# Sending each token of two mixture layers to its own expert, in blocks of 64, through DRAM

## The reference

```
x = x + _L0_gnn_ref(xn, ...) + _L0_mix_ref(xn[None], ...)[0]
x = x + _L0_ffn_ref(_layernorm(x), ...)          # mixture, erf gelu, bias on the logits
...
x = x + _L2_gnn_ref(...) + _L2_mix_ref(...)
x = x + _L2_ffn_ref(_layernorm(x), ...)          # mixture, silu

def _L0_ffn_ref(x, Ws, bs, W1, b1, W2, b2):      # E = 8 experts, D = 768, F = 384, 512 tokens
    logits = xt @ Ws + bs
    probs = jax.nn.softmax(logits, axis=-1)
    routes, prob_max = jnp.argmax(probs, -1), jnp.max(probs, -1)
    h = gelu(jnp.einsum('td,edf->etf', xt, W1) + b1[:, None, :], approximate=False)
    y = jnp.einsum('etf,efd->etd', h, W2) + b2[:, None, :]
    out = jnp.take_along_axis(y, routes[None, :, None], axis=0)[0]
    return out * prob_max[:, None]
```

## Time and profile before

| | |
|---|---|
| median of three runs | 5067.96 us (5066.04 to 5071.9) |
| the profiled execution | 5071.08 us, its span 5069.0 us |
| TensorE busy | 4789.0 us, 94% |
| VectorE busy | 980.5 us |
| ScalarE busy | 988.2 us |
| granted TensorE clock, mean | 0.967 |
| DMA | 716.13 MB, 141 GB/s over the span |

### The profile page before, as it was taken

The page is one execution under the profiler, slowest core; times in us unless marked ns, Lnnn a source line. Parts: engine busy times, 40 slices in busy tenths (PEclk is TensorE's granted clock), DMA queues, the critical chain, the costliest instruction groups (busy, mean ns, idle before and its releaser), DMA issues.

```text
span 5069.0 us, 39557 instructions
## 1 busy us (share of the span) xinstructions
PE 4789.0 (94%) x15392; PEld 2191.0 (43%) x15410; DVE 980.5 (19%) x1791; ACT 988.2 (19%) x1796; POOL 54.1 (1%) x91
## 2 busy tenths in 40 slices
PE   8999999999999998998999999999779999999998
PEld 6544444444444544443444444444333433333343
DVE  3782111212101133212300000010443100000000
ACT  0121112323201425331210101010541111010010
POOL 1000000000000000000000000000000000000000
PEclk9999999999899998999999999989889999999999
DMA  3013222121232121012203030323104899999998
GB/s 115 1 39 103 75 70 73 52 71 58 62 100 75 46 67 33 25 50 83 71 31 102 29 99 32 105 72 99 29 25 148 344 410 423 411 424 410 417 414 358
DMA packets 110479, 716.13 MB, mean 141 GB/s; under 512 B 13200, under 2 KB 13392, under 8 KB 71552
## 3 DMA queue, kind: packets, MB, share of 16 engines
q1 hardware_dynamic: 103104, 670.21, 35.6%
q0 software_dynamic: 5216, 25.34, 1.3%
q10 hardware_dynamic: 2016, 18.49, 0.9%
HBM read 707.18 MB, written 6.82 MB: 141 GB/s over the span
## 4 chain that ended last, share of the span: by engine, by line
PE 88%; DVE 4%; DMA 4%; ACT 3%; issue 1%; SPq 0%; ACTq 0%; DVEq 0%
PE bank L392 80%; DMA mem<-in_experts 4%; PE bank L546 3%; PE bank L513 2%; PE bank L390 2%; DVE rstd L1715 1%; DVE mem L1950 0%; ACT mem L1402 0%; DVE mem L1946 0%; ACT mem L1557 0%; ACT mem L1423 0%; DVE mem L1718 0%; ACT mem L1123 0%; DMA mem<-in_edges 0%; ACT mem L1265 0%
## 5 line engine op out<-in xcount | busy, mean ns | idle before, releaser
L392 PE MATMUL bank<-mem 128*128 128x512 f32 (+5 forms) x11616 | 3942.9, 568 | 115.9 <-DMA mem<-in_experts 25.9
L392 PEld LDWEIGHTS bank<-mem 128*128 128x128 f32 (+3 forms) x11616 | 1668.8, 172 | 2320.9 <-issue 2160.2
L1123 ACT ACTIVATE mem<-bank,cols 128x512 f32<-128x512 f32 (+1 forms) x139 | 95.5, 687 | 975.5 <-PE bank L392 975.5
L390 PE MATMUL bank<-ident,mem 128*128 128x128 f32 (+2 forms) x1300 | 200.2, 309 | 59.2 <-ACT mem L1402 9.9
L390 PEld LDWEIGHTS bank<-ident,mem 128*128 128x128 f32 (+2 forms) x1300 | 167.9, 160 | 151.6 <-issue 91.4
L1123 ACT ACTIVATE mem<-bank 128x512 f32<-128x512 f32 x168 | 99.5, 597 | 551.6 <-PE bank L392 547.0
L546 PE MATMUL bank<-mem 128*128 128x512 bf16 x798 | 177.5, 381 | 1.2 <-issue 0.3
L1725 DVE TENSOR_TENSOR mem<-mem,EV 128x512 f32<-128x512 f32 x42 | 29.1, 693 | 587.6 <-ACT EV L1134 587.6
L2216 DVE TENSOR_TENSOR mem<-mem,EV 128x512 f32<-128x512 f32 x48 | 33.2, 692 | 552.2 <-ACT EV L1652 552.2
L392 PE MATMUL bank<-mem,ones 128*128 128x512 f32 (+1 forms) x232 | 111.2, 653 | 26.5 <-ACT mem L1157 17.3
L546 PEld LDWEIGHTS bank<-mem 128*128 128x128 bf16 x816 | 79.7, 98 | 99.1 <-issue 3.5
(11 more groups left out here) (283 smaller groups left out, 1915.8 us busy)
## 6 DMA issues: line engine op xcount, KB each, us to landing
mem<-in_experts SPq DMA_DIRECT2D x282, 1536.0 KB, 12.2
mem<-in_weights SPq DMA_DIRECT2D x426, 512.0 KB, 3.5
mem<-in_weights POOLq DMA_DIRECT2D x36, 384.0 KB, 7.7
mem<-in_experts ACTq DMA_DIRECT2D x6, 1536.0 KB, 14.5
mem<-in_feats ACTq DMA_DIRECT2D x3, 2048.0 KB, 23.1
scratch<-mem POOLq DMA_DIRECT2D x5, 1024.0 KB, 5.1
mem<-scratch POOLq DMA_DIRECT2D x5, 1024.0 KB, 8.2
mem<-in_feats ACTq DMA_DIRECT2D x1, 2560.0 KB, 36.5
```

The costliest lines, as they stand in the source:

```text
L390: ins = nc.tensor.transpose(out, lhsT, ident[0:lhsT.shape[0], 0:lhsT.shape[0]])
L392: ins = nc.tensor.matmul(out, lhsT, rhs, start=start, stop=stop)
L1123: nc.scalar.activation(dst(m), src[0:width, :], func, scale=scale, **how).then_inc(bank_free.sem, bank_free.tick((label, m)))
```

## The change

Both mixture layers are written anew; the other layers keep their code. For each mixture:

1. The logits are taken as rows: 6 matmuls with the gate weights as stationary operand, then 4 small ones that turn them into tokens by experts. The argmax gives `comb`, a one-hot of the chosen expert. Matmuls with `before_me` (a triangle of ones) and `ones` count, for each token, how many tokens before it chose the same expert.
2. The first 64 tokens of expert e get the slots of block e. Tokens past 64 get slots in 7 overflow blocks, handed out to the experts in order. 15 blocks of 64 slots hold 512 tokens whatever the routing. A chain of small VectorE instructions works out the slot of each token and, for each overflow block, the number of its expert.
3. `XN` is transposed to token rows (24 transposes); GpSimd scatters the rows to their slots in a DRAM buffer with 4 indirect DMAs and loads the slots back, in three plain DMAs.
4. Two blocks at a time make one of 8 sets (the eighth has one block). A set is transposed (6), goes through its two experts' first weights (`up`: 12 matmuls of 64 rows by 384), bias on VectorE, activation on ScalarE, 3 transposes, the second weights (`down`: 12 matmuls of 64 rows by 384, in two banks), bias on VectorE.
5. Each set's result is written to a second DRAM buffer; at the end 4 indirect DMAs gather the rows of the tokens, VectorE and ScalarE scale them by the gate (two each), and 24 transposes bring them back to features by tokens for `residual`.

The weights of a block come as halves of 1.125 MB (`up`: 3 KB rows; `down`: 1.5 KB rows) in a ring of six, `moe_w`, loaded by SyncE. With each `up` half come two biases, each loaded to 64 partitions (`moe_b1`, 1.5 KB rows; `moe_b2`, 512 B rows). For overflow blocks SyncE reads the expert's number from SBUF first. `moe_b1` is first put in DRAM at the start of the program. SyncE's loop over the weight ring becomes a list, with the two mixtures' loads in between.

Besides: after the last sum of squares of each norm but `ln0`, TensorE does 5 matmuls of 128x512 into bank 5 that nobody reads (`FILL`). At the start GpSimd sets more constants and writes zeros to the 8 sets of the DRAM buffer.

```diff
+BLOCK, OVER = 64, 7
+FILL = 5
...
+        moe_order = [("up", 0), ("up", 1)]
+        for p in range(SETS):
+            moe_order.append(("down", p))
+            if p + 2 < SETS:
+                moe_order.append(("up", p + 2))
+        moe_halves = [(kind, b) for kind, p in moe_order for b in (2 * p, 2 * p + 1) if b < BLOCKS]
...
+            def moe_loads(tag, source):
...
+                sp.wait_ge(dve_done.sem, dve_done.at((source, KC - 1)))
...
+                for n, (kind, b) in enumerate(moe_halves):
+                    p, rows = b // 2, slice(BLOCK * (b % 2), BLOCK * (b % 2) + BLOCK)
+                    if n >= 6:
+                        as_kind, as_b = moe_halves[n - 6]
+                        sp.wait_ge(agg_done.sem, agg_done.at((tag, as_kind, as_b // 2)))
+                    if b == ME and kind == "up":
+                        sp.wait_ge(dve_done.sem, dve_done.at((tag, "over")))
+                    slot = moe_w[n % 6]
+                    if kind == "up":
+                        expert = b if b < ME else sp.value_load(over_i[0:1, 0, b - ME:b - ME + 1], min_val=0, max_val=ME - 1)
+                        one = slice(b, b + 1) if b < ME else bass.ds(expert, 1)
+                        sp.dma_start(slot.rearrange("p (t n) -> p t n", t=3),
+                                     up[one].rearrange("a p t n -> (a p) t n")).then_inc(moe_w_in[n % 6], 16)
+                        if p >= 2:
+                            sp.wait_ge(dve_done.sem, dve_done.at((tag, "h", p - 2)))
+                        sp.dma_start(moe_b1[p % 2][rows, :], b1[one].to_broadcast([BLOCK, MF])).then_inc(moe_b1_in[p % 2], 16)
+                        if p >= 2:
+                            sp.wait_ge(dve_done.sem, dve_done.at((tag, "y", p - 2, 1)))
+                        sp.dma_start(moe_b2[p % 2][rows, :].rearrange("p (m f) -> p m f", m=KC),
+                                     b2[one].to_broadcast([BLOCK, KC, P])).then_inc(moe_b2_in[p % 2], 16)
...
@@ gpsimd
+            def moe(tag):
+                nth = 1 + (tag == "moe2")
+                pool.wait_ge(dve_done.sem, dve_done.at((tag, "slots")))
+                pool.wait_ge(bank_free.sem, bank_free.at((tag, "rows", KC - 1)))
+                for t in range(NT):
+                    pool.indirect_dma_start(out=by_slot, out_offset=bass.IndirectOffsetOnAxis(ap=slot_i[:, t:t + 1], axis=0),
+                                            in_=moe_rows[:, t, :], in_offset=None).then_inc(rows_out, 16)
+                pool.wait_ge(rows_out, 16 * NT * nth)
+                for n, (start, stop) in enumerate([(0, 1), (1, 4), (4, SETS)]):
+                    pool.dma_start(slot_rows[n // 2][:, start % 4:(stop - 1) % 4 + 1, :],
+                                   by_slot[start * P:stop * P, :].rearrange("(q s) d -> s q d", s=P)).then_inc(slots_in[n], 16)
+                for p in range(SETS):
+                    rows = rows_of(p)
+                    pool.wait_ge(dve_done.sem, dve_done.at((tag, "y", p, 1)))
+                    pool.dma_start(y_by_slot[p * P:p * P + rows, :], moe_y[p % 2][0:rows, :]).then_inc(y_out[p % 2], 16)
...
@@ tensor, norm_sums
+                for k in range(FILL if label != "ln0" else 0):
+                    mm(bank[5][:, :], ones[:, :], sq[:, k, :])
...
@@ tensor, experts_of_one
+                slots_t(0)
+                up(0)
+                slots_t(1)
+                up(1)
+                for p in range(SETS):
+                    hidden_t(p)
+                    if p + 2 < SETS:
+                        slots_t(p + 2)
+                    down(p)
+                    if p + 2 < SETS:
+                        up(p + 2)
```

More of the change, by code:

```diff
@@ L658, in experts_of_one, with rows @@
             def experts_of_one(tag, ln, source, gate, gate_bias):
+                nth = 1 + (tag == "moe2")
+                blocks = [(t, m) for t in range(NT) for m in range(KC)]
+                def rows(n):
+                    out = open_bank()
+                    for j, (t, m) in enumerate(blocks[4 * n:4 * n + 4]):
+                        ins = mm(out[:, j * P:(j + 1) * P], XN[:, m, t * P:(t + 1) * P], None, last=j == 3, transpose=True)
+                    ins.then_inc(bank_full.sem, bank_full.tick((tag, "rows", n)))
@@ L660, in experts_of_one @@
                 norm_sums(ln, XT, after(dve_done, source))
[L661 removed]
                 out = open_bank()
+                for k in range(KC):
+                    pe.wait_ge(dve_done.sem, dve_done.at((ln, k)))
+                    ins = mm(out[0:ME, :], gate[:, k, :], XN[:, k, :], k == 0, k == KC - 1, k == KC - 1)
+                ins.then_inc(bank_full.sem, bank_full.tick((tag, "logit_rows")))
+                rows(0)
+                rows(1)
@@ new lines, in experts_of_one @@
+                v.tensor_tensor(slot, rank, first, ALU.add).then_inc(dve_done.sem, dve_done.tick())
+                follow()
+                v.scalar_tensor_tensor(over, rank, float(BLOCK), over, ALU.is_ge, ALU.mult).then_inc(dve_done.sem, dve_done.tick())
+                follow()
+                v.tensor_tensor(slot_i[:, :], slot, over, ALU.add).then_inc(dve_done.sem, dve_done.tick((tag, "slots")))
+                number, pair, odd, past = (over_f[:, n, :] for n in range(4))
+                v.tensor_tensor(counted[0:1, 0:OVER, :].rearrange("p a b -> p (a b)")[:, 0:0 + OVER * OVER].rearrange("p (n e) -> p n e", n=OVER),
+                                so_far[0:1, 0:OVER].rearrange("p (a e) -> p a e", a=1).to_broadcast([1, OVER, OVER]),
+                                over_number[:, :].rearrange("p (n a) -> p n a", a=1).to_broadcast([1, OVER, OVER]), ALU.is_le).then_inc(
+                                    dve_done.sem, dve_done.tick())
```

350 lines of the change are left out of this document (283 added, 67 removed).

## The result

The changed kernel takes 4918.07 us (median of 4 runs, 4916.25 to 4918.29), the kernel before 5068.95: a ratio of 0.9702, 95% interval 0.9685 to 0.9718. The forecast was 4873 with 4820 to 4962: right in direction and inside its range, 45 us too fast. The profiled execution took 4918.29 us with a span of 4916.3; TensorE is busy 4466.9 us of it (91%), 322 less than before. The chain of the page answers to the earlier trace rows; these are shares of the span by engine.

A forecast was written before the change was run, and what follows sets the result against it. TensorE was taken to bound the kernel (88% of the chain). From the profiled 5071.1 us, mixtures took off 185.2, fillers 14.5, small things added 4.5: 4875.9; the median 3.1 lower, said as 4873, range 4820 to 4962.

The forecast's parts named there:

- A: Start of each mixture, tokens to slots: logits, transposes, counting matmuls and VectorE steps, 17.0 us.
- B: Scatter to DRAM slots and load back: four indirect DMAs at 1.3 us each, landing, load, transposes; 13.7 us.
- C: From the first `up` to the end of set 0: 17.0 us.
- D: Five rounds between set results, held by SyncE's order: 19.9 us each plus 2.1 for expert-number reads, 101.6 us.
- E: The last two sets: `down(6)` waits 11.9 us for its halves, then `down(7)` finds its weights loaded; 21.6 us.
- F: Way back: result write, four gathers, scaling, transposes, residual adds and partial sums; 20.8 us.
- Rival 4: GpSimd goes row by row in the 16 indirect DMAs; at 0.15 us a row 5159 us, slower than before; chance 0.07.
- Rival 3: Short rows are dear in the weight and bias loads: round 31.8 us, about +74 each mixture, 5021 us; chance 0.09.
- Rival 2: Weights run ahead, rounds bound by transfer alone at 14.9 us: each mixture 25 us shorter, 4823 us; chance 0.07.
- Rival 1: TensorE stays at 1.2 GHz through the blocks: round 26.6 us, +43 for each mixture, 4960 us; chance 0.18.
- The fillers and small things: Matmuls behind norms keep the clock up, net gain 14.5 us; idled TensorE, GpSimd constants, zeros and biases cost 4.5.

The follow-up runs named there:

- odd_first: Changed kernel with SyncE's wait for the set's result kept, but the odd `up` half issued before the two `moe_b2` loads: 4933.6 us.
- b2_rows: Changed kernel with the same bytes of `moe_b2` loaded as 64 rows of 3 KB from an input of its own, not 384 of 512 B: 4891.7 us.
- thin_bias: Changed kernel with each bias load from set 2 on cut to one row to one partition, so not the reference's result: 4883.7 us.
- gate_only: Changed kernel with 9216 B weight rows, one-row biases added by matmul, no fillers at `lny`; SyncE's wait still ahead of the odd half: 4887.1 us.
- ungated: Changed kernel with the `moe_b2` load and its wait for the set's result moved behind the weights of the next `down`: 4837.5 us.

## Why the prediction was right, and where it was off

By its own terms, for the first mixture (us):

| term | forecast | measured |
|---|---|---|
| A, tokens to slots | 17.0 | 14.1 |
| B, DRAM way | 13.7 | 13.6 |
| C, to the end of set 0 | 17.0 | 17.8 |
| D, five rounds | 101.6 | 122.4 |
| E, last two | 21.6 | 27.8 |
| F, way back | 20.8 | 21.2 |
| sum | 191.7 | 216.9 |

- **B and F, the indirect DMAs**: 1.0 us each on GpSimd (estimate 1.3, bounds 0.54 and 3.0), landing after 4.7 and 4.2 us. Rival 4 is out. The Trainium skill ("GPSIMD Engine Reference", Performance pitfalls for Q7 kernels), whose 102 cycles per small read I had turned into an estimate of 11 us, does not describe this transfer: the trace shows 0.95 to 1.07 us for 128 rows.

```profile
1297.13 1.07 POOL L459 DMA_INDIRECT by_slot<-mem,slot_i  x1 [258.38 <-DVE counted L2201]
```

- **D, the step that was mis-sized**: "TensorE idles to 7.0 (the odd half's landing)" and "3 halves of 1.18 MB, biases 0.5 MB and the written result 0.39 MB, 4.43 MB, at 419 GB/s 10.6 us; the short rows 1.1". The order on SyncE and the path were right, the transfer times on it were not. The odd half landed at 11.3, +4.3, and the first `up` took 7.0 instead of 6.6: 19.9 + 4.3 + 0.4 = 24.6, and 24.5 is measured. TensorE waited 11.9 us before `up` where the forecast said 5 to 6. The other way to `down`, all its loads landed, had been put at 14.4 and ended at about the same moment, for `down` started 19.2 to 20.5 after each result, in four rounds of five straight from a wait for DMA: `odd_first` shows it: with the odd half there at 6.7, `down` still started at 19.4. So the term that was too small is the whole transfer between a result and the next `down`, not only its first half. Of the 2.1 us for the reads of expert numbers about 1 shows: the three rounds with reads take 24.6 in the mean, the two without 24.3. The 419 GB/s had been read off a stream of 12 KB rows. The halves came in 3 KB and 1.5 KB rows at 350 to 390, and while the bias loads' 512 B rows went, at 222. The window of the earlier trace rows in which a 512 B-row load "barely lowered" the rate had one such load in 1.5 MB tiles; here two stood ahead of and beside the one half that TensorE waited for. `b2_rows` and `thin_bias` show this part (26 and 34 us, 24 and 23 in the mixtures), `gate_only` that with long rows and hardly any biases the working gives 21.1 where 21.8 is measured. The landing itself was put 1.3 to 2.0 us too early, as `gate_only` shows; that `odd_first` met the 7.0 is no proof of it, since the forecast had a bias load ahead of the odd half and this run has none.
- **E** was 6.2 longer, a wait behind the gate once more: `down(6)` started 15.4 us after the result and not 11.9, and then took 6.9 us at a low clock for a part, where 4.6 had been put.
- **Rival 3** (short rows are dear, 0.09) named this mechanism, but priced a row as one of a full engine: 31.8 us a round. The truth lay between it and mine, nearer to mine; its sign, a share near 1 with under 250 GB/s, showed in the stretch at 222 GB/s. **Rival 2** (weights run ahead) was rightly small: the gate was real, and `ungated` shows what taking it away brings, 81 us (72 in the mixtures) from 4918 rather than the 50 from 4873 that I gave it. **Rival 1**: the clock is 0.50 in most of `up` and 1.00 in `down`, as forecast (the clock column of the six windows above).
- **That the total fell inside the range** owes something to its width: it reached up to rival 1 and so covered an error of 48 us in the mixtures that had another cause.

- **A** was 2.9 shorter: the eviction (0.59 us) ran beside the first transposes, the counting matmuls took 1.9 us instead of 3.0 and the VectorE steps behind them 2.2 instead of 2.9, and of the other 16 transposes 0.4 stuck out and not 1.3.
- **The fillers and small things**: outside the mixtures the profiled runs differ by 15.6 us (4918.29 - 5071.08 = -152.8, less the mixtures' -137.2), forecast 14.5 - 4.5 = 10.0. The gain behind a norm was rightly sized: 2.5 and 2.7 us for 2.6. The windows behind `lnh` and TensorE at `lny`, which answer to the earlier trace rows:

```profile
504.00:507.00 3.00, 3.00 (x8) 1.32 (x7) 1.41 (x3) 2.94 (x5) 0.00 (x0) 1.00 0.00 0
```

```profile
1737.58 11.40 PE L518 MATMUL bank<-mem,ones 128*128 128x512 f32 x22 [1.45 <-ACT mem L1366]
...
1748.82 31.06 PE L518 MATMUL bank<-mem 128*128 128x512 f32 x72
```

  At `lny` I had read only that no wait follows the sums, and charged 4.3 us. The kernel before waits a little later, behind the next 24 matmuls; that wait takes the fillers up, and after the change 36 matmuls run through. The row of the kernel before:

```profile
1850.86 7.70 PE L392 MATMUL bank<-mem 128*128 128x512 f32 x14 [3.43 <-ACT mem L1123]
```

  In eight traces with the fillers `lny` to `ln3` is 504.5 to 505.6 us; before it is 505.3, and without fillers at `lny` 504.6 and 505.7. In the changed kernel and in `b2_rows` it is 509, since a stretch at the low clock some 140 us behind `lny` lasts longer there, and in `thin_bias` 497, with less of it; what decides on that stays open. Differences of 5 to 12 us between totals can come from there alone.
- **The sum**: mixtures 48.0 us too hopeful, the rest 5.6 too gloomy, 42.4 together: 4918.3 against 4875.9.

## What to carry to other kernels

A rate is read from rows of the shape that will be moved, and for each wait on its own: price what stands ahead of and beside the first transfer that is waited for, and then what the last one needs. `odd_first` mended only the first and lost 15 us. Read a change of some ten us from the stretch that was changed, not from the total alone. A wait placed ahead of prefetches in an in-order queue turns a ring into no ring; put the load that must wait last, and send a broadcast operand as one row and let TensorE spread it. A filler or an added instruction is charged only after looking past the next group for a wait that takes it up.
